# Attention inside a decoder kernel: minus the row maximum is transposed to two places in PSUM, and ScalarE and VectorE copy it to the queries

## The reference, cut to what matters

```python
Q = proj(query, wq_w, wq_b)
K = proj(key, wk_w, wk_b)
V = proj(value, wv_w, wv_b)
scale = 1.0 / np.sqrt(HEAD_DIM).astype(np.float32)
scores = jnp.einsum('bhqd,bhkd->bhqk', Q, K) * scale
causal = jnp.tril(jnp.ones((S, S), dtype=bool))
scores = jnp.where(causal, scores, -jnp.inf)
attn = jax.nn.softmax(scores, axis=-1)
out = jnp.einsum('bhqk,bhkd->bhqd', attn, V)
```

## Time and profile before

| what | us |
|---|---|
| median of 3 runs | 659.65 |
| lowest, highest | 658.91, 660.65 |
| the profiled execution | 660.65 |
| its span, first to last instruction | 658.9 |
| TensorE busy | 577.2 (88%) |
| VectorE busy | 380.2 (58%) |
| ScalarE busy | 275.8 (42%) |
| POOL busy | 186.3 (28%) |

### The profile page before, as it was taken

The page is one execution under the profiler, slowest core; times in us unless marked ns, Lnnn a source line. Parts: engine busy times, 40 slices in busy tenths (PEclk is TensorE's granted clock), DMA queues, the critical chain, the costliest instruction groups (busy, mean ns, idle before and its releaser), DMA issues.

```text
span 658.9 us, 11028 instructions
## 1 busy us (share of the span) xinstructions
PE 577.2 (88%) x3856; PEld 333.5 (51%) x3856; DVE 380.2 (58%) x792; ACT 275.8 (42%) x460; POOL 186.3 (28%) x231
## 2 busy tenths in 40 slices
PE   6899999999979889989999988850499999999994
PEld 3648586655834535555464444320144554545581
DVE  5874737333176767685697767069633433434645
ACT  4260512425046656666667657500043333333204
POOL 3133232061123123121222222110234444342233
PEclk9999999999989899999999989985699999999998
DMA  8696000013530641155025731049179999999873
GB/s 264 212 381 239 0 0 0 1 67 98 163 94 0 186 119 49 49 178 176 17 91 166 228 157 65 0 154 422 35 270 386 395 395 397 402 392 391 273 268 128
DMA packets 43583, 120.38 MB, mean 183 GB/s; under 512 B 6212, under 2 KB 28308, under 8 KB 40468
## 3 DMA queue, kind: packets, MB, share of 16 engines
q1 hardware_dynamic: 38372, 113.20, 47.5%
q0 software_dynamic: 4320, 6.03, 4.2%
q10 hardware_dynamic: 848, 0.60, 0.3%
HBM read 95.88 MB, written 21.83 MB: 179 GB/s over the span
## 4 chain that ended last, share of the span: by engine, by line
PE 72%; DVE 11%; ACT 7%; DMA 4%; issue 3%; SPq 1%; POOL 1%; ACTq 0%; DVEq 0%; POOLq 0%
PE PS L2026 13%; PE PS L1697 8%; PE PS L1706 8%; PE PS L1782 4%; PE PS L1862 4%; PE PS L1849 4%; PE PS L1823 4%; PE PS L2058 4%; PE PS L2039 4%; DVE Mx L1133 2%; ACT arena L1506 2%; PE PS L1801 2%; PE PS L1666 2%; PE PS L1819 2%; PE PS L1774 2%
## 5 line engine op out<-in xcount | busy, mean ns | idle before, releaser
L1133 DVE TENSOR_REDUCE Mx<-PS 128x1 f32<-128x384 f32 (+3 forms) x176 | 103.6, 634 | 40.0 <-PE PS L1823 38.7
L1518 ACT ACTIVATE arena<-PS 128x512 f32<-128x512 f32 (+1 forms) x176 | 90.3, 559 | 48.1 <-PE PS L1849 46.7
L797 POOL TENSOR_SCALAR_AFFINE_SELECT arena<-arena 128x512 f32<-128x512 f32 x64 | 40.9, 638 | 165.0 <-ACT arena L1518 165.0
L1849 PE MATMUL PS<-arena 108*128 108x512 bf16 (+3 forms) x256 | 62.3, 306 | 11.7 <-ACT arena L1506 5.7
L1823 PE MATMUL PS<-arena 96*128 96x128 bf16 (+3 forms) x256 | 62.8, 303 | 0.0
L1697 PE MATMUL PS<-arena 128*128 128x512 f32 x128 | 56.1, 593 | 3.2 <-ACT arena L1423 1.6
L1706 PE MATMUL PS<-arena 128*128 128x256 f32 x256 | 55.9, 379 | 0.0
L1635 PE MATMUL PS<-ident,identb 128*128 128x512 bf16 x82 | 23.7, 434 | 33.2 <-DVE Y L1258 29.3
L1300 DVE COPY X<-PS 128x512 f32<-128x512 f32 x24 | 16.6, 691 | 61.6 <-PE PS L2026 61.6
L1706 PEld LDWEIGHTS PS<-arena 128*128 128x128 f32 x256 | 48.6, 190 | 6.6
L1590 ACT ACTIVATE X<-X 128x512 f32<-128x512 f32 x48 | 29.4, 630 | 52.7 <-DVE X L1307 52.6
(11 more groups left out here) (217 smaller groups left out, 966.5 us busy)
## 6 DMA issues: line engine op xcount, KB each, us to landing
ring_a<-experts SPq DMA_DIRECT2D x12, 2048.0 KB, 15.5
arena<-experts SPq DMA_DIRECT2D x12, 2048.0 KB, 16.5
arena<-pieces SPq DMA_DIRECT2D x192, 64.0 KB, 2.3
ring_a<-experts SPq DMA_DIRECT2D x12, 512.0 KB, 14.9
sums<-zrow SPq DMA_DIRECT2D x3, 2048.0 KB, 20.1
arena<-experts SPq DMA_DIRECT2D x12, 512.0 KB, 16.0
pieces<-arena SPq DMA_DIRECT2D x4, 768.0 KB, 3.9
pieces<-ring_a SPq DMA_DIRECT2D x4, 768.0 KB, 3.7
```

Source lines behind the costliest of these rows:

```text
L797: pool.affine_select(out=pb[j % 2][:, :, 0:P], in_=pb[j % 2][:, :, 0:P], compare_op=ALU.is_ge, fill=0.0, base=0, pattern=[[0, GH], [1, P]] ...
L1133: dve.tensor_reduce(Mx[:, g % 2, i, heads[0]:heads[-1] + 1], bank(score_banks[(g * NSH + u) % 3])[:, 0:len(heads) * w] .rearrange("p (h n) ...
L1518: act.activation(pb[j % 2][:, heads[0]:heads[-1] + 1, 0:w], bank(exp_banks[(g * NSH + n) % 2])[:, 0:len(heads) * w] .rearrange("p (h n) -> ...
L1849: mm = pe.matmul(bank(exp_banks[(g * NSH + n) % 2])[:, a * w:(a + 1) * w], KTs[0:SX, g * GH + h, j * P:(j + 1) * P], QTs[0:SX, g * GH + h, ...
```

## The change

Minus the maximum is written twice into nst, 32 columns apart (`twin`), with zeros around it from a new constant `memset`, and one transpose of 44 columns per query tile puts it into rows 64 to 75 and 96 to 107 of bank 5. ScalarE copies rows 96 to 107 for the first head of the group only, 12x512. VectorE copies rows 64 to 75 into rows 96 to 107 of QTs for the second head (12x512) and for the third and fourth together (12x1024). The first shifted product waits for ScalarE's copy, the second and the third for VectorE's first and second (semaphore nted), and whoever takes bank 5 next waits for both engines. In `negate` three of the four operations write 32 numbers per partition, and the third is now a copy of Mr that waits for the second. VectorE's copies come in slot j = 3 after list 1 and ahead of list 2, in turnover (0, 0) ahead of `ln_out_norm`. `value` in slot (3, 3) moves from list 0 to list 2 on all engines.

```diff
--- before.py
+++ after.py
@@ -29,6 +29,7 @@
 NPR = 6
 SK = NPR * HD
 SX = SK + GH * NPC
+SN = SK - 32
 K_PIECES = (0, 1, 2, 0, 1, 0)
 Q_PIECES = (0, 0, 0, 1, 1, 2)
 NRD = len(K_PIECES) + len(Q_PIECES)
@@ -85,7 +86,7 @@
     (2, 1): ([], [("norm", 0, -1)], [], [("heads", 0, 0)]),
     (2, 3): ([], [("turn", 0, -1), ("turn", 1, -1)], [], []),
     (3, 0): ([("logits", 0, -1)], [], [], []),
-    (3, 3): ([("value", 1, 1)], [], [], []),
+    (3, 3): ([], [], [("value", 1, 1)], []),
 }
 IN_TIME = sorted((g + NG * -ahead, j, n, m, name, k, ahead) for (g, j), lists in TASKS.items()
                  for n, names in enumerate(lists) for m, (name, k, ahead) in enumerate(names))
@@ -176,7 +177,7 @@
         causal = sb("causal", [P, P], BF16)
         Mx = sb("Mx", [P, 2, TT, GH])
         Mr = sb("Mr", [P, TT, GH])
-        nst = sb("nst", [P, 2, TT, GH, NPC], BF16)
+        nst = sb("nst", [P, 2, TT, 2, SK - SN], BF16)
         own = sb("own", [P, GH])
         zrow = sb("zrow", [P, D])
         rden = sb("rden", [P, TT, GH])
@@ -368,7 +369,8 @@
         mxs = signal("mxs", NG * NSH)
         mneg = signal("mneg", NG * 4)
         ntp = signal("ntp", NG)
-        nte = signal("nte", NG * 2)
+        nte = signal("nte", NG)
+        nted = signal("nted", NG * 2)
         stm = signal("stm", NG * NSH)
         exq = signal("exq", NG * NSH)
         msk = signal("msk", NG * TT)
@@ -434,7 +436,7 @@
         b2_split = sem("b2_split")
         b2_out = sem("b2_out")
         VALUES, CHOSEN, SHIFTED, ROWS, WEIGHED, TOPK = 22, 31, 33, 34, 39, 40
-        CONSTS, SETUP, ANGLES = 11, 10, 9
+        CONSTS, SETUP, ANGLES = 12, 10, 9
 
         def final_sum(b, t):
 
@@ -696,6 +698,7 @@
             const(pool.memset(mhalf[:], -0.5))
             const(pool.memset(zrow[:], 0.0))
             const(pool.memset(decay, 1.0))
+            const(pool.memset(nst[:], 0.0))
             const(pool.iota(ph_i, pattern=[[1, C]], base=0, channel_multiplier=0))
             settle()
             for m in (ident, identb):
@@ -1080,7 +1083,7 @@
             ln_out(B - 2)
             ln_out_norm(B - 2)
 
-            for g in (vev, ksd, qsd, mxs, mneg, odv, ln4):
+            for g in (vev, ksd, qsd, mxs, mneg, nted, odv, ln4):
                 dve.sem_inc(g.s, g.per)
             dve.wait_ge(rows_in, 16)
             dve.tensor_reduce(own[SK:SX, :], ident[SK:SX, SK:SX]
@@ -1135,20 +1138,35 @@
                                       .rearrange("p (h n) -> p h n", h=len(heads)),
                                       AX.X, ALU.max).then_inc(mxs.s, 1)
 
+            def twin(g, c):
+
+                return nst[:, g % 2, :, :, 0:SX - SK]\
+                    .rearrange("p i d (h c) -> p i d h c", c=NPC)[:, :, :, :, c]
+
             def negate(b, g):
 
-                m, d = Mx[:, g % 2], nst[:, g % 2]
+                m = Mx[:, g % 2]
+                twice_m, twice_r = (v.unsqueeze(2).to_broadcast([P, TT, 2, GH]) for v in (m, Mr[:]))
+                d = [twin(g, c) for c in range(NPC)]
                 dve.wait_ge(mxs.s, mxs.now(b, NSH * (g + 1)))
                 dve.wait_ge(ntp.s, ntp.now(b, g - 1) if g >= 2 else ntp.before(b, NG + g - 1))
-                dve.tensor_scalar(d[:, :, :, 0], m, -1.0, None, ALU.mult).then_inc(mneg.s, 1)
+                dve.tensor_scalar(d[0], twice_m, -1.0, None, ALU.mult).then_inc(mneg.s, 1)
                 dve.wait_ge(mneg.s, mneg.now(b, 4 * g + 1))
-                dve.scalar_tensor_tensor(Mr[:], m, -1.0, d[:, :, :, 0], ALU.mult, ALU.subtract)\
+                dve.scalar_tensor_tensor(Mr[:], m, -1.0, d[0][:, :, 0, :], ALU.mult, ALU.subtract)\
                     .then_inc(mneg.s, 1)
-                dve.scalar_tensor_tensor(d[:, :, :, 1], m, -1.0, d[:, :, :, 0], ALU.mult,
-                                         ALU.subtract).then_inc(mneg.s, 1)
+                dve.wait_ge(mneg.s, mneg.now(b, 4 * g + 2))
+                dve.tensor_copy(d[1], twice_r).then_inc(mneg.s, 1)
                 dve.wait_ge(mneg.s, mneg.now(b, 4 * g + 3))
-                dve.tensor_tensor(d[:, :, :, 2], Mr[:], d[:, :, :, 1], ALU.subtract)\
-                    .then_inc(mneg.s, 1)
+                dve.tensor_tensor(d[2], twice_r, d[1], ALU.subtract).then_inc(mneg.s, 1)
+
+            def dve_minus_max(b, g):
+
+                rows = slice(SK, SX)
+                dve.wait_ge(ntp.s, ntp.now(b, g + 1))
+                negated = spare(0).bitcast(BF16)[SN:SN + SX - SK, 0:T]
+                dve.tensor_copy(QTs[rows, GH * g + 1, :], negated).then_inc(nted.s, 1)
+                dve.tensor_copy(QTs[rows, GH * g + 2:GH * g + 4, :], wide(negated, 2))\
+                    .then_inc(nted.s, 1)
 
             def divide(b, g):
 
@@ -1202,6 +1220,8 @@
                     divide(*prev)
                 dve_do(steps[1])
                 maxima(then, shares[1])
+                if j == TT - 1 and then is not None:
+                    dve_minus_max(*then)
                 dve_do(steps[2])
                 maxima(then, shares[2])
                 if j == 2 and then is not None:
@@ -1216,6 +1236,7 @@
                 for banks in share:
                     maxima((0, 0), banks)
             negate(0, 0)
+            dve_minus_max(0, 0)
             ln_out_norm(B - 1)
             slots(0, dve_slot, first=True)
             for b in range(1, B - 1):
@@ -1502,10 +1523,8 @@
             def minus_max(b, g):
 
                 act.wait_ge(ntp.s, ntp.now(b, g + 1))
-                for m in range(2):
-                    act.activation(QTs[SK:SX, GH * g + 2 * m:GH * g + 2 * m + 2, :],
-                                   wide(spare(0).bitcast(BF16)[SK:SX, 0:T], 2), ACT.Copy)\
-                        .then_inc(nte.s, 1)
+                act.activation(QTs[SK:SX, GH * g, :], spare(0).bitcast(BF16)[SK:SX, 0:T], ACT.Copy)\
+                    .then_inc(nte.s, 1)
 
             def exponentials(b, g, j):
                 w = T - j * P
@@ -1748,11 +1767,15 @@
 
             read_by = {0: None, 1: None}
 
+            negated_by_dve = []
+
             def take(k, sig, value):
 
 
                 if read_by[k % 2] is not None:
                     pe.wait_ge(*read_by[k % 2])
+                if k % 2 == 0 and negated_by_dve:
+                    pe.wait_ge(nted.s, negated_by_dve.pop())
                 read_by[k % 2] = (sig.s, value)
                 return spare(k)
 
@@ -1828,18 +1851,22 @@
 
             def minus_max(b, g):
                 pe.wait_ge(mneg.s, mneg.now(b, 4 * (g + 1)))
-                o = take(0, nte, nte.now(b, 2 * g + 2)).bitcast(BF16)
+                o = take(0, nte, nte.now(b, g + 1)).bitcast(BF16)
+                negated_by_dve.append(nted.now(b, 2 * g + 2))
                 for i in range(TT):
-                    mm = pe.transpose(o[SK:SX, i * P:(i + 1) * P],
-                                      nst[:, g % 2, i].rearrange("p h c -> p (h c)"), identb[:])
+                    mm = pe.transpose(o[SN:SX, i * P:(i + 1) * P],
+                                      nst[:, g % 2, i].rearrange("p d n -> p (d n)")[:, 0:SX - SN],
+                                      identb[:])
                 mm.then_inc(ntp.s, 1)
 
             def shifted(b, g, j):
 
                 w = T - j * P
                 for n, heads in enumerate(SHARED[j], FIRST[j]):
-                    if j == 0 and heads[0] % 2 == 0:
-                        pe.wait_ge(nte.s, nte.now(b, 2 * g + heads[0] // 2 + 1))
+                    if j == 0 and heads[0] == 0:
+                        pe.wait_ge(nte.s, nte.now(b, g + 1))
+                    elif j == 0 and heads[0] < 3:
+                        pe.wait_ge(nted.s, nted.now(b, 2 * g + heads[0]))
 
                     if n >= 2 or g > 0:
                         pe.wait_ge(exq.s, exq.now(b, g * NSH + n - 1))
```

## The result

The changed kernel takes 663.64 us (median of 10 runs, 662.04 to 667.36) against 660.91 (10 runs, 658.91 to 664.44) for the kernel before: ratio 1.0042, 95% interval 1.0022 to 1.0063. That is 2.7 us slower. Forecast was 1.0 us slower, with "same" as the likeliest outcome (0.44, against 0.34 for slower); the time lies in the range, on the side of two of the slower rivals (663.4 and 662.9). The forecast of 660.6 started from a median of three runs, 659.65; with ten runs that median is 1.3 us higher. The profiled execution took 664.11, its span is 661.6 against 658.9.

A forecast was written before the change was run, and what follows sets the result against it. TensorE, busy 216 of 243 us in the attention stage, bounds it; 27 us can be won. Gains 2.13, 1.1, 0.81, 0.18 less losses 0.2, 1.0, 1.6, 1.45, 1.0 make -1.03: 660.6 us, range 656.4 to 665.0.

The forecast's parts named there:

- two of the slower rivals (663.4 and 662.9): Extra low-clock stretches in two turnovers, 663.4; negate's copy waiting 0.6 for POOL at six places, 662.9; together chance 0.23.
- VectorE's pair by bytes: VectorE's two PSUM copies, priced by bytes, take 0.48 and 0.69 us, together ending 1.1 us after the turnover's transposes.
- The rival of the element price: VectorE copies one element per cycle, the pair ends at +1.9, 5.7 us on top: 666.3; chance 0.12.
- The plain turnovers: At (0, 3) and (3, 0), earlier first and third products gain 1.2 and 1.15, less 0.22: 2.13 us.
- (1, 0) and (2, 0): Turnovers preparing group 0 of batches 1 and 2: gain 0.55 us each, from TensorE's 0.41 and the wait before `heads_out`.
- (1, 1) and (2, 1): Line 1097 waits behind VectorE's copies, ends +1.85 us after the transposes instead of +1.02, delaying `heads`: loss 0.8 each.
- (2, 2) and (2, 3): VectorE's queue loses 1.15 us, negate 0.05 and 0.22, against 0.41 gained in (2, 3): loss 1.0.
- (0, 0): Turnover opening the attention stage: statistics start at +1.1, first maximum at +5.9 instead of +4.3; loss 0.8, with negate 1.0.
- the pieces at (1, 3): VectorE's queue at (1, 2) delays the last key piece 1.4 us, for which TensorE waits: both turnovers lose 1.45.
- `negate`: Third operation held to POOL's end, fourth after it: 0.22 us later, counted fully at six places (bounds 0.05 and 0.6).
- (3, 2): Copies, line 1173 and statistics make the first maximum 1.1 us later against a VectorE pause of 0.9: loss 0.2.
- more low clock: Longer TensorE idling in five turnovers; two bring a 1.4 us stretch each: 663.4; chance 0.23 together with a longer negate.

The follow-up runs named there:

- x4: The changed kernel with the `memset` of nst behind all other constants and outside TensorE's count: 663.83 us, ratio 1.0041 to the kernel before.
- x6: The changed kernel, but ScalarE alone makes all copies and `negate` writes one place as before: 660.58 us, ratio 0.9995 to the kernel before.
- S: The changed kernel, but ScalarE makes all copies (12x1024 twice) and VectorE none; new layout and longer `negate` remain: 664.51 us, ratio 1.0044 to the kernel before.
- x12: The changed kernel, but where group 1 is opened VectorE evacuates the query's second half before the copies: 663.72 us, ratio 1.0012 to the kernel before.
- x11: The changed kernel with `value` in slot (3, 3) put back from list 2 to list 0: 668.49 us, ratio 1.0103 to the kernel before.
- S1: The same kernel as x6, by its column in the table of steps: ScalarE copies everything, `negate` as before; 660.58 us, ratio 0.9995.
- x8: The changed kernel with two `scalar_tensor_tensor` that don't wait, one per place, instead of the copy in `negate`: 664.35 us, ratio 1.0052 to the kernel before.
- M: The changed kernel, but VectorE copies only at groups 0 and 3, without (0, 0); ScalarE copies all elsewhere: 657.34 us, ratio 0.9934 to the kernel before.
- R: The changed kernel, but VectorE copies only at groups 1 and 2 and at (0, 0); ScalarE copies all elsewhere: 669.33 us, ratio 1.0117 to the kernel before.
- x9: The changed kernel, but at the very first turnover ScalarE copies all four heads: 663.25 us, ratio 1.0026 to the kernel before.

## Why the prediction was right or wrong

**Right: prices and gains.** *VectorE's pair by bytes:* forecast 0.48 and 0.69, measured 0.424 and 0.680; it ends at +1.06, forecast +1.1. The rival of the element price is out. The Trainium skill's estimate (VectorE: DVE Perf Modes) was 0.39 and 0.66; the measured ones lie between it and mine, 0.03 and 0.02 above the page's. *ScalarE's copy* 0.60 forecast, 0.590. *The plain turnovers:* -2.13 forecast for (0, 3) and (3, 0), -1.85 measured. (1, 0) and (2, 0): -1.1 and -1.62, mis-sized: I took 0.15 of the wait before `heads_out`. (3, 3): -0.41 and -0.83, counted for its first product only, though the third is 0.82 earlier too (+3.12, before +3.94). *`memset`, wider transposes:* nothing forecast, nothing measured (x4, x6).

**Right: the queue behind VectorE's wait, where it was followed by rows.** (1, 1) and (2, 1): line 1097 (1100 after) was forecast to end at +1.85, it ends at 267.04, +1.85; `heads` was forecast at +2.0, it starts at +1.99. That is 0.83 later than before (the first product at +2.46 for +1.63), and 0.8 was forecast. The other 0.15 of the step is `negate`'s: with ScalarE copying it vanishes here, as `heads` waits for VectorE's evacuation at the same absolute time (S: first product at +1.48), with VectorE's copies in between it doesn't. x12 shows mechanism and place. (2, 2) and (2, 3): +1.0 forecast, +1.07.

**(0, 0): right without the clock.** Statistics at +1.10 and the first maximum at +6.0 (forecast +1.1 and +5.9). The loss of 0.8 was chosen as half of 1.6; the step without a stretch of low clock is +1.10 (x11), 0.14 of it the next `negate`, so 0.96. The kernel before had a stretch there itself, but S1, without it, takes the same time for the step (0.00), so that one cost nothing. What the forecast lacked is the stretch at 197.76, 1.24 us.

**Wrong: the pieces at (1, 3).** "Together lose 1.45, whatever is won between." The step (1, 2) alone is +1.34, but (1, 3) then won 0.76. The last piece was made 3.08 us later (it ends at 286.19, line 1111, against 283.11, line 1108), yet the pieces landed at 298.44 against 297.56, only 0.88 later, and TensorE came to the place 1.35 us after them, at 299.79. Two things had changed. The last of the twelve transfers that TensorE waits for there was issued 2.83 us later (295.86, before 293.03) but took 2.58 us and not 4.53; its neighbours take some 2.5 in both kernels. And TensorE was late itself. This is the changed kernel's chain at that place:

```profile
283.65 0.68 DVE arena L1168
...
284.36 0.69 DVE ring_a L1191
285.05 0.06 DVE arena L1111
...
286.10 1.41 DVE stats L923 x4
...
288.02 0.57 DVE Mx L1136
288.60 0.79 DVE arena L1122 x4
289.39 1.20 DVE Mx L1136 x2
```

No DMA is in it where the earlier trace rows had one. I had added VectorE's delay to the landing and left TensorE where it was; but the same queue on VectorE, by way of the maxima, had made TensorE late already. And I had taken 4.54 us as what the transfer costs, where it was slow in that one trace: with 4.53 us it would have landed at 300.39, 0.6 us after TensorE's place. Of the 0.76, 0.47 is gone in S1 too (there the transfer took 3.80), where nothing of that place is edited. The sign that I had named, the first scores waiting over 0.5 us for the pieces, didn't come. Sum of the two turnovers: +0.58 instead of +1.45, the one term that came out much better.

**Half right: `negate`.** "0.22 us later" at six places. It is 0.25 longer, for the reason given (the third held to POOL's end, the fourth after it). Columns S and S1 differ at eleven steps without low clock by 1.5 us together: 0.25 at (1, 2), (2, 2), (3, 2), which is `negate` of (1, 3), (2, 3), (3, 3), all three counted; nothing at (1, 1) and (2, 1), where I had said that TensorE is behind it anyway; but also 0.09 to 0.14 at (0, 0), (1, 0), (1, 3), (2, 0) and (2, 3), where I had counted nothing. There "elsewhere more" was wrong by a little. So the step that failed is the list of places, by some 0.6 us. In the times it is more, 3.2 us; what is over 1.7 goes with the lower clock of S's runs, which the forecast didn't tie to `negate`. The Trainium skill (SBUF — State Buffer, "SBUF: two separate sides") also names VectorE's instructions with two inputs in SBUF as ones shut out by a POOL operation that reads SBUF, as the mask does; x8's, held for 0.63 us, agrees.

**Wrong: (3, 2).** 0.42 forecast with the next `negate`, 0.94 measured: 0.28 is `negate` (S and M), as forecast, and 0.66 are the copies, for which I had 0.2. I set 1.1 us of lateness against a pause of 0.9. The pause was used as I had thought; the lateness was mis-sized. VectorE's first maximum, before and after (+2.39 and +4.02), and the small operations ahead of it:

```profile
399.76 0.66 DVE L1133 TENSOR_REDUCE Mx<-PS 128x4 f32<-128x512 f32 x1
...
403.84 0.62 DVE L927 BATCH_NORM_AGGREGATE mv<-stats 128x2 f32<-128x6 f32 x4
...
404.38 1.89 DVE L1136 TENSOR_REDUCE Mx<-PS 128x4 f32<-128x512 f32 x3
```

That is 1.6 us later, not 1.1: the evacuation ahead (line 1173, after 1191) starts at +1.10 instead of -0.28, which is 1.38, and the four of line 927 take 0.62 us instead of 0.38. In R they take 0.38, and there the copies cost 0.38 instead of 0.66. Why the fourth of them is late in the changed kernel isn't shown.

**Half open: the clock.** Rival "more low clock" gave 663.4. In the profiled execution three stretches of 3.41 us at 0.5 before became five (two side by side at 184.11, then 197.76, 225.07 and 385.49). One of them:

```profile
197.76:201.17 3.41, 3.37 (x17) 1.10 (x16) 2.64 (x6) 1.47 (x3) 0.63 (x1) 0.50 0.00 0
```

Its price is seen in the steps: steps that differ only in such a stretch differ by 1.24 us (x11 and the changed kernel at (0, 0)), 1.50 (x11, (1, 2)), 1.62 (x12, (2, 2)), 1.64, 1.05 and 1.67 (x9, (0, 2), (0, 3) and (2, 1)), where I took 1.4; the one at (0, 0) in the kernel before cost nothing. How many come isn't the kernel's alone: the profiles of six kernels in which VectorE copies at fifteen or sixteen turnovers have 5, 6, 5, 5, 6 and 2 of them in the stage, those of the six with fewer such turnovers or none, leaving R out, 3, 4, 4, 3, 4 and 3, R has 5. One profile of each can't show that the change brings them, though the means (4.8 and 3.5) times 1.4 would be 1.8 us. The clocks of all runs say more. The 64 runs of those six kernels have 0.9601 on the mean, the 77 of the kernel before 0.9625, a difference of 0.0025 with an interval of 0.0014 to 0.0035: about 1.1 us of time. The ten of the changed kernel alone (0.9610) don't stand clear of 0.9625. By the fit the changed kernel's 2.5 us of mean span are 1.8 at one clock and 0.7 of clock, so that rival was right in part. What lowers the clock isn't shown: S, where VectorE copies nothing, has 0.9595, and M 0.9636.

So the sum of the steps is +3.1 against +1.0 forecast. Measured less forecast: +0.5 on the way to (0, 0), where x9 and x11 are at +0.01 and -0.04 and the profiles with a long stretch at 183 to 190 at +0.36 to +0.60, so probably the clock, though x4 has +0.38 with no stretch there; +1.5 at (0, 0), 1.24 of it the clock; +0.7 at (3, 1), in a step with low clock in both kernels; +0.5 at (3, 2); +0.4 at (1, 1) and (2, 1); -0.9 at (1, 2) and (1, 3); -0.5 at (1, 0) and (2, 0); -0.4 at (3, 3); the rest within 0.25 each, +0.2 together. Of the 3.1 us 0.4 is back by the end of the span (+2.7). The time came near the forecast partly by luck, because errors of both signs cancelled: without the clock, the terms above are wrong by about -2.0 and +1.5. The chances leaned the right way only in part: slower had 0.34, less than no difference.

## What to carry to other kernels

Moving a copy to another engine moves a wait with it: list, place by place, what stands behind it in that engine's queue and who waits for that, and choose the engine by place. Here the same copies won about 1 us at five turnovers and lost about 1 us at five others, and choosing by place, with the short `negate` where ScalarE copies alone, turned +0.4% into -0.9%. When a delay is set against something in the old trace, such as a late transfer, check that the change doesn't move the other side too, and that what was late there is late in a second trace. And compare the clocks of the runs before a difference of times is put down to an edit.

## What the runs showed of the hardware

VectorE copies 12x512 bf16 from PSUM in 424 ns and 12x1024 in 680, ScalarE in 590 and 1009: an element more costs 0.50 ns on VectorE and 0.82 on ScalarE. A VectorE instruction on 16 or 32 elements that otherwise takes 0.19 to 0.23 us took 0.49 to 0.63 when POOL's mask had been running for 0.1 us or more, whether it was a copy with conversion (line 1158), one with two inputs (line 1150 before) or x8's `scalar_tensor_tensor`, and ended within 0.05 us of the mask. Most unedited steps of different kernels agree within 0.04 us where the clock is the same, a few differ by 0.1 to 0.3, so one profile of each shows a difference of some 0.3 us at one place, where the medians of 12 runs resolve about 1.3 (0.2%). And runs of one kernel whose mean granted clock is 0.001 lower are 0.44 us longer.
